# Where the operands of the products stand in SBUF: z's parts on even 64-byte lines, the key sums' parts on odd ones

## The chip, the cores and the metric

The kernel runs on one core of a Trainium2 chip. The metric is the device time of one execution in microseconds; the time before is the median of three runs. One further execution was profiled, and all rows come from that one.

## The reference

A graph layer, a linear-attention layer and a mixture of experts over 12500 nodes of 256 channels, in float32:

```python
xn = _layernorm(x)
x = x + gnn(xn, edges) + mix(xn)
x = x + ffn(_layernorm(x))
# gnn: xt = xn @ W; softmax over heads of gathered sums; weighted xt[col]
# mix: Q, K = elu(xn @ Wq) + 1, elu(xn @ Wk) + 1
#      KV = sum over nodes of K * v;  msg = (Q @ KV) / (Q . sum K) @ Wm, normalized
#      h = relu(concat(xn, msg) @ W1) @ W2;  mix = xn + layernorm(h)
# ffn: shared = relu(relu(y @ sW1 + b) @ sW2 + b) @ sW3 + b
#      4 experts of two hidden layers (eW1, eW2) and eW3, the best two weighted by a softmax
```

## The kernel before

**Tiling.** The 12500 nodes are cut into 25 groups (NG) of 512 nodes (GR), four row tiles of 128 each; the last group has two. Every large product is done in two-part float32r: a value is split into a high part (`..._hi`) and the rest (`..._lo`), and `split_mm` (L268 to L274) issues three matmuls for it, high x high (L272), high x low (L273), low x high (L274). The first argument of `pe.matmul` after the output is the operand that is loaded and held in the array (128 columns), the second the one that moves through it.

**Two kinds of product.** In one, a slice of the weights is held and 512 columns of nodes move: `hidden` (L541) and `w1_part` (L579). So run Wq and the first half of W1 on xT, the second half of W1 on mT (the message), sW1 and the four eW1 on z (the normalized middle result), sW2 on s1. In the other, 128 nodes are held and 256 columns move: W2 (`w2_pair`, L650) and eW3 (L745) with h held, sW3 (L740) with s2 held and out_bias (L739) with scaleT held, each against the weights, and `p2_m` (L569) with z held against g, the key sums folded with Wm. In profile rows the moving operand is named first: `psum<-z_hi,w_hi` has w_hi held and z_hi moving, `psum<-w_hi,h_hi` has h_hi held.

**Stages.** Phase 1 (L532) runs over the groups for the keys, the key sums and the gather table. Phase 2 (L680) is the second pass: one turn i works on three groups at a time, on the queries of group i (Wq, denominators, p2_m), the hidden layer of group i - 1 (W1, W2) and the experts of group i - 2. TensorE's order within a turn is written out by hand: transposes of row_n, W1's x half on the old xT buffer, outputs 2 and 3 (12 matmuls), Wq on the new one (12), W1's message half (12, then transposes of row_z, then 12), sW1, logits, denominators, sW1, eW1 (6 + 6 + 24 on z), W2 (48), sW2 (6), the second expert layer (8), the gates spread by gate_sel (2), p2_m (24), W1's x half for the next turn, outputs 0 and 1, on the new xT (12), the output stage (40). Every engine waits on semaphores; the other engines follow TensorE within the turn. There are two xT buffers, `xT_hi[0]`/`xT_lo[0]` (xT0) and `xT_hi[1]`/`xT_lo[1]` (xT1), used in turn; they are loaded by DMA from a table.

**Layout.** SBUF tiles are stacked one after another by `sb` (L70). It counts 64-byte lines per partition in `used[0]`; a tile with a `side` begins on a line whose number has that parity, if need be behind a filling line of 64 bytes:

```python
lines = -(-4 * math.prod(shape[1:]) // LINE)
if side is not None and used[0] % 2 != side:
    stack.enter_context(nc.sbuf_tensor(name + "_side", [P, LINE // 4], F32))
    used[0] += 1
made = stack.enter_context(nc.sbuf_tensor(name, shape, dt))
...
used[0] += lines
```

MOVING is 0 and HELD is 1. The weights w_hi and w_lo are on side 0, h, s2 and scaleT on side 1. z is on side 1 before, g on side 0; xT, s1, mT, gate_sel, den_sel and rdenT have no side of their own and stand where the tiles before them end. Starts in bytes per partition, added up from the tile sizes in the order of allocation:

| tile | before | within 256 | after | within 256 |
|---|---|---|---|---|
| w_hi / w_lo | 512 / 25088 | 0 | the same | 0 |
| gate_sel | 50688 | 0 | 50752 | 64 |
| second_w | 51968 | 0 | 52032 | 64 |
| g_hi / g_lo | 52992 / 55040 | 0 | 53056 / 55104 | 64 |
| xT_hi0 / xT_lo0 | 74880 / 78976 | 128 | 75008 / 79104 | 0 |
| xT_hi1 / xT_lo1 | 126976 / 131072 | 0 | 127104 / 131200 | 128 |
| row_n / row_z | 70784 / 88512 | 128 / 192 | 70848 / 88640 | 192 / 64 |
| e1 | 104896 | 192 | 105024 | 64 |
| s2_hi / s2_lo | 113088 / 178240 | 192 / 64 | 113216 / 178624 | 64 / 192 |
| den_sel / rdenT | 87488 / 115904 | 192 / 192 | 87616 / 116032 | 64 / 64 |
| h_hi / h_lo | 135232 / 143424 | 64 | 135360 / 143552 | 192 |
| z_hi / z_lo | 151616 / 155712 | 64 | 151808 / 155904 | 0 |
| s1_hi / s1_lo | 159808 / 163904 | 64 | 160000 / 164096 | 0 |
| scaleT | 168000 | 64 | 168256 | 64 |
| mT_hi / mT_lo | 170048 / 174144 | 64 | 170368 / 174464 | 128 |

Slices within a tile begin at multiples of 512 bytes, so each has its tile's place within 256.

Of the kernel before, what the change touches and what calls it, by code (L numbers as in the profile page):

```python
# [7 lines left out]
F32R = mybir.dt.float32r  # L8
# [6 lines left out]
C = 256  # L15
# [5 lines left out]
P = 128  # L21
R = 128
T = 4
GR = R * T
# [4 lines left out]
CK = C // P  # L29
BANK = 512  # L30
LINE, HALF_LINE = 64, 32
MOVING, HELD = 0, 1
XT_W = C + HEADS
XA_W = XT_W + HEADS
KX_W = C + 2
# [28 lines left out]
def gps_layer(nc, A):  # L64

    ctx = ExitStack()
    with ctx:
        used = [0]

        def sb(name, shape, dt=F32, stack=ctx, side=None):  # L70
# [6 lines that stand above are left out]
            if -(-4 * math.prod(shape[1:]) // HALF_LINE) % 2:  # L77
                stack.enter_context(nc.sbuf_tensor(name + "_fill", [P, HALF_LINE // 4], F32))
            used[0] += lines
            return made  # L80
# [46 lines left out]
        w_hi = sb("w_hi", [P, W_TOTAL], F32R, side=MOVING)  # L127
        w_lo = sb("w_lo", [P, W_TOTAL], F32R, side=MOVING)
        out_bias = sb("out_bias", [P, C], F32R, side=MOVING)
        gate_sel = sb("gate_sel", [P, 2, P], F32R)  # L130
        gate_w = sb("gate_w", [P, CK, QUAD])
        second_w = sb("second_w", [P, EXPERTS, HEAD_CH])
        g_hi = sb("g_hi", [P, CK, C], F32R, side=MOVING)
        g_lo = sb("g_lo", [P, CK, C], F32R, side=MOVING)
        g2_bc = sb("g2_bc", [R, C])
        b2_bc = sb("b2_bc", [R, C])
        h_bias = sb("h_bias", [P, 4])
# [29 lines left out]
        ctx0.close()  # L167
        used[0] = before_ctx0
        row_n = sb("row_n", [R, T, C])
        xT_hi0 = sb("xT_hi0", [P, CK, GR], F32R)  # L170
        xT_lo0 = sb("xT_lo0", [P, CK, GR], F32R)
        qf = sb("qf", [P, CK, GR])
        idx = [sb(f"idx{n}", [R, 2, T], I32) for n in range(2)]
        low_rows = sb("low_rows", [P, QUAD + 1])
        den_sel = sb("den_sel", [P, CK, P], F32R)

        ctx1, before_ctx1 = ExitStack(), used[0]
# [36 lines left out]
        s2_hi = sb("s2_hi", [P, GR], F32R, side=HELD)  # L215
        pad = sb("pad", [P, P])
        kden = sb("kden", [P, CK, QUAD])
        rdenT = sb("rdenT", [P, GR], F32R)
        rden_hi = sb("rden_hi", [P, R + 1], F32R)
        xg = [sb(f"xg{n}", [R, T, XT_W]) for n in range(2)]  # L220
        ag = [sb(f"ag{n}", [R, T, HEADS]) for n in range(2)]
        xT_hi = [xT_hi0, sb("xT_hi1", [P, CK, GR], F32R)]
        xT_lo = [xT_lo0, sb("xT_lo1", [P, CK, GR], F32R)]
        h_hi = sb("h_hi", [P, 4, GR], F32R, side=HELD)
        h_lo = sb("h_lo", [P, 4, GR], F32R, side=HELD)
        z_hi = sb("z_hi", [P, CK, GR], F32R, side=HELD)
        z_lo = sb("z_lo", [P, CK, GR], F32R, side=HELD)
        s1_hi = sb("s1_hi", [P, 2, GR], F32R)
        s1_lo = sb("s1_lo", [P, 2, GR], F32R)
        scaleT = sb("scaleT", [P, GR], F32R, side=HELD)  # L230
        mT_hi = sb("mT_hi", [P, CK, GR], F32R)
        mT_lo = sb("mT_lo", [P, CK, GR], F32R)
        s2_lo = sb("s2_lo", [P, GR], F32R, side=HELD)
        relu = [sb(f"relu{n}", [P, 2, GR]) for n in range(3)]
        gb_bc = sb("gb_bc", [R, EXPERTS])
# [1712 lines left out]
```

## Time and profile before

| what | value |
|---|---|
| median of 3 runs | 1325.66 us (1324.2 to 1329.84) |
| profiled execution | 1322.97 us, span 1321.1 us |
| TensorE (PE) busy | 1292.3 us, 98% |
| weight loads (PEld) busy | 1119.4 us |
| VectorE / ScalarE / GpSimd busy | 1105.4 / 733.8 / 770.7 us |
| matmuls | 8812 |
| one turn of phase 2 | 42.6 us, 22 turns |

Times are microseconds, means in a group nanoseconds. PE is the matmul engine, PEld its weight loads, which overlap with the matmuls. A matmul's duration includes its way through the array, so that consecutive ones overlap; the distance from one start to the next is the rate.

### The profile page before, as it was taken

How to read it: one execution, taken by the hardware profiler on the slowest of the kernel's cores; microseconds unless marked ns; L12 is line 12 of the kernel's file. 1: busy time of each engine (PE TensorE's matmuls, PEld its weight loads, DVE VectorE, ACT ScalarE, POOL GpSimd, SP SyncE). 2: the span in 40 equal slices, each digit the busy share in tenths (PEclk: the TensorE clock that was granted, in tenths of full speed). 3: DMA queues.
4: the chain of work that ended last, by engine and by line, in shares of the span. 5: the costliest groups of instructions: out<-in, count | busy, mean ns of one | idle time of the engine just before them, and what ended most of it. 6: DMA issues, size and time to landing. Idle time of an engine off the chain costs nothing.

```text
span 1321.1 us, 26301 instructions
## 1 busy us (share of the span) xinstructions
PE 1292.3 (98%) x8812; PEld 1119.4 (85%) x8812; DVE 1105.4 (84%) x2597; ACT 733.8 (56%) x1332; POOL 770.7 (58%) x815
## 2 busy tenths in 40 slices
PE   6999999899999999999999999999999999999998
PEld 5999999876888888888888888888888888888876
DVE  6988777978888888888888888888888888888875
ACT  4555555345645655455645655555645655555654
POOL 5777777745546654655556564655555654655531
PEclk9999999899999999999999999999999999999999
DMA  6787766523212221222111221222111221212000
GB/s 206 245 283 253 251 226 223 165 61 73 65 42 60 77 75 29 76 60 80 50 54 56 80 73 32 76 60 80 44 60 56 80 72 32 76 60 71 26 17 23
DMA packets 65459, 123.23 MB, mean 93 GB/s; under 512 B 31725, under 2 KB 36176, under 8 KB 65422
## 3 DMA queue, kind: packets, MB, share of 16 engines
q1 hardware_dynamic: 57422, 109.25, 25.6%
q0 software_dynamic: 8000, 13.53, 4.8%
q8 instruction: 19, 0.31, 0.1%
q14 instruction: 18, 0.15, 0.0%
HBM read 70.41 MB, written 52.32 MB: 93 GB/s over the span
## 4 chain that ended last, share of the span: by engine, by line
PE 88%; DVE 4%; issue 3%; POOL 2%; DVEq 1%; POOLq 1%; ACT 1%; ACTq 0%
PE psum L272 26%; PE psum L273 25%; PE psum L274 25%; PE psum L484 5%; PE psum L676 3%; PE psum L729 1%; PE psum L667 1%; PE psum L566 1%; PE psum L739 1%; PE psum L559 1%; POOL h_lo L1841 1%; POOL ag L1837 0%; POOLq L1775 0%; POOL xg L1835 0%; DVE kf L1249 0%
## 5 line engine op out<-in xcount | busy, mean ns | idle before, releaser
L1841 POOL TENSOR_TENSOR h_lo<-relu,h_hi 128x1024 fp32r<-128x1024 f32 (+1 forms) x50 | 119.8, 2397 | 142.1 <-ACT h_hi L998 142.0
L272 PE MATMUL psum<-w_hi,h_hi 128*128 128x256 f32 x588 | 164.4, 280 | 1.6 <-POOL h_lo L1841 1.5
L273 PE MATMUL psum<-w_lo,h_hi 128*128 128x256 f32 x588 | 163.8, 278 | 0.0
L274 PE MATMUL psum<-w_hi,h_lo 128*128 128x256 f32 x588 | 163.7, 278 | 0.0
L1841 POOL TENSOR_TENSOR s_lo<-relu,s_hi 128x512 fp32r<-128x512 f32 (+1 forms) x45 | 82.5, 1834 | 95.8 <-ACT s_hi L1099 94.3
L272 PE MATMUL psum<-z_hi,w_hi 128*128 128x512 f32 (+1 forms) x300 | 121.6, 405 | 2.0 <-DVE z_lo L1611 1.1
L1835 POOL DMA_INDIRECT xg<-table_xt,idx x100 | 99.5, 995 | 34.9 <-issue 31.9
L272 PE MATMUL psum<-xT_hi,w_hi 128*128 128x512 f32 (+1 forms) x300 | 119.4, 398 | 0.1
L997 ACT ACTIVATE relu<-psum,h_bias 128x512 f32<-128x512 f32 (+1 forms) x100 | 67.8, 678 | 88.5 <-PE psum L274 88.4
L273 PE MATMUL psum<-xT_lo,w_hi 128*128 128x512 f32 (+1 forms) x300 | 116.9, 390 | 0.0
L274 PE MATMUL psum<-xT_hi,w_lo 128*128 128x512 f32 (+1 forms) x300 | 116.7, 389 | 0.0
L273 PE MATMUL psum<-z_lo,w_hi 128*128 128x512 f32 (+1 forms) x300 | 116.6, 389 | 0.0
L274 PE MATMUL psum<-z_hi,w_lo 128*128 128x512 f32 (+1 forms) x300 | 116.2, 387 | 0.0
L272 PEld LDWEIGHTS psum<-w_hi,h_hi 128*128 128x128 f32 x588 | 110.4, 188 | 3.5 <-POOL h_lo L1841 1.9
L1837 POOL DMA_INDIRECT ag<-table_al,idx x100 | 95.2, 952 | 30.5 <-issue 30.5
L274 PEld LDWEIGHTS psum<-w_hi,h_lo 128*128 128x128 f32 x588 | 111.4, 190 | 0.0
L273 PEld LDWEIGHTS psum<-w_lo,h_hi 128*128 128x128 f32 x588 | 110.5, 188 | 1.0
L915 ACT ACTIVATE row_n<-psum,nm_m,rs_m 128x256 f32<-128x256 f32 x98 | 47.4, 564 | 111.4 <-POOL nm_m L1778 111.4
L1470 DVE SCALAR_TENSOR_TENSOR base<-xb,rn,b_bc 128x256 f32<-128x256 f32 x98 | 91.7, 975 | 0.2 <-issue 0.2
L1009 ACT ACTIVATE e<-psum,e_bias 128x512 f32<-128x512 f32 (+1 forms) x100 | 67.3, 676 | 37.2 <-PE psum L274 37.1
L272 PE MATMUL psum<-mT_hi,w_hi 128*128 128x512 f32 (+1 forms) x200 | 80.1, 401 | 0.9 <-DVE mT_lo L1619 0.9
L1811 POOL TENSOR_TENSOR k_lo<-kf,k_hi 128x1024 fp32r<-128x1024 f32 x25 | 63.0, 2521 | 30.3 <-DVE k_hi L1253 30.3
(274 smaller groups left out, 4298.1 us busy)
## 6 DMA issues: line engine op xcount, KB each, us to landing
xb<-in_x SPq DMA_DIRECT2D x47, 448.0 KB, 3.5
xT_hi_table<-x1T_hi SPq DMA_DIRECT2D x25, 512.0 KB, 2.8
xT_lo_table<-x1T_lo SPq DMA_DIRECT2D x25, 512.0 KB, 3.6
xT_hi<-xT_hi_table SPq DMA_DIRECT2D x25, 512.0 KB, 3.8
xT_lo<-xT_lo_table SPq DMA_DIRECT2D x25, 512.0 KB, 4.7
table_xt<-xts SPq DMA_DIRECT2D x24, 455.0 KB, 3.0
out<-xmid SPq DMA_DIRECT2D x24, 448.0 KB
xb<-in_x SPq DMA_DIRECT2D x47, 64.0 KB, 3.6
```

Source lines behind the costliest of these rows:

```text
L272: pe.matmul(out, wh, xh, start=first, stop=False)
L273: pe.matmul(out, wh, xl, start=False, stop=False)
L274: return pe.matmul(out, wl, xh, start=False, stop=last)
L484: last = pe.transpose(psum[:, b + c, j * R:(j + 1) * R], src[:, j, c * P:(c + 1) * P], ident[0:R, 0:R])
L915: act.activation(out[:, j, :], src(j), ACT.Identity, bias=nm[which][:, j:j + 1], scale=rs[which][:, j:j + 1]).then_inc(S[done], 1)
L997: act.activation(out[:, 0:t * R], colT(b, t=t), ACT.Relu, bias=bias)
L1009: act.activation(e1[:, e, 0:t * R], colT(bank, t=t), ACT.Relu, bias=e1_bias[:, e:e + 1]).then_inc(S["e1_relu"], 1)
L1470: last = stt(base[:, j, :], xb[par][:, j, :], rn2[par][:, 0, j:j + 1], b2_bc[:], ALU.mult, ALU.add)
L1811: ptt(k_lo[par][:], kf[par][:], k_hi[par][:], ALU.subtract).then_inc(S["k_split"], 1)
L1835: pool.indirect_dma_start(xg[par][:, j, :], None, table_xt.ap(), bass.IndirectOffsetOnAxis(idx[par][:, 1, j:j + 1], 0)).then_inc(S[f"gath{ ...
L1837: pool.indirect_dma_start(ag[par][:, j, :], None, table_al.ap(), bass.IndirectOffsetOnAxis(idx[par][:, 0, j:j + 1], 0)).then_inc(S[f"gath{ ...
L1841: ptt(out, src, hi, ALU.subtract).then_inc(S[done], 1)
```

## The change

It gives sides to tiles that had none and exchanges two. z_hi and z_lo go to side 0 and g_hi and g_lo to side 1; xT, s1 and mT are put on side 0, gate_sel, den_sel and rdenT on side 1. Filling lines come in or fall away, so that nearly all tiles behind gate_sel start 64 to 384 bytes later. No instruction is added, removed or reordered.

```diff
-MOVING, HELD = 0, 1
+MOVING, HELD, G_SIDE = 0, 1, 1
-        gate_sel = sb("gate_sel", [P, 2, P], F32R)
+        gate_sel = sb("gate_sel", [P, 2, P], F32R, side=HELD)
-        g_hi = sb("g_hi", [P, CK, C], F32R, side=MOVING)
-        g_lo = sb("g_lo", [P, CK, C], F32R, side=MOVING)
+        g_hi = sb("g_hi", [P, CK, C], F32R, side=G_SIDE)
+        g_lo = sb("g_lo", [P, CK, C], F32R, side=G_SIDE)
-        xT_hi0 = sb("xT_hi0", [P, CK, GR], F32R)
-        xT_lo0 = sb("xT_lo0", [P, CK, GR], F32R)
+        xT_hi0 = sb("xT_hi0", [P, CK, GR], F32R, side=MOVING)
+        xT_lo0 = sb("xT_lo0", [P, CK, GR], F32R, side=MOVING)
-        den_sel = sb("den_sel", [P, CK, P], F32R)
+        den_sel = sb("den_sel", [P, CK, P], F32R, side=HELD)
-        rdenT = sb("rdenT", [P, GR], F32R)
+        rdenT = sb("rdenT", [P, GR], F32R, side=HELD)
-        xT_hi = [xT_hi0, sb("xT_hi1", [P, CK, GR], F32R)]
-        xT_lo = [xT_lo0, sb("xT_lo1", [P, CK, GR], F32R)]
+        xT_hi = [xT_hi0, sb("xT_hi1", [P, CK, GR], F32R, side=MOVING)]
+        xT_lo = [xT_lo0, sb("xT_lo1", [P, CK, GR], F32R, side=MOVING)]
-        z_hi = sb("z_hi", [P, CK, GR], F32R, side=HELD)
-        z_lo = sb("z_lo", [P, CK, GR], F32R, side=HELD)
-        s1_hi = sb("s1_hi", [P, 2, GR], F32R)
-        s1_lo = sb("s1_lo", [P, 2, GR], F32R)
+        z_hi = sb("z_hi", [P, CK, GR], F32R, side=MOVING)
+        z_lo = sb("z_lo", [P, CK, GR], F32R, side=MOVING)
+        s1_hi = sb("s1_hi", [P, 2, GR], F32R, side=MOVING)
+        s1_lo = sb("s1_lo", [P, 2, GR], F32R, side=MOVING)
-        mT_hi = sb("mT_hi", [P, CK, GR], F32R)
-        mT_lo = sb("mT_lo", [P, CK, GR], F32R)
+        mT_hi = sb("mT_hi", [P, CK, GR], F32R, side=MOVING)
+        mT_lo = sb("mT_lo", [P, CK, GR], F32R, side=MOVING)
```

## Rows read from the trace of the kernel before

**Rows 1.** The page, sections 1 and 2: busy time; span in 40 slices.
```profile
...
PE 1292.3 (98%) x8812; PEld 1119.4 (85%) x8812; DVE 1105.4 (84%) x2597; ACT 733.8 (56%) x1332; POOL 770.7 (58%) x815
...
PEclk9999999899999999999999999999999999999999
...
```

**Rows 2.** Waits of PE: waiter, releaser, total us, times, longest.
```profile
...
PE psum L600 <- ACT xn L915: 9.2, 1, 9.2
PE psum L633 <- DVE kx L1359: 1.8, 1, 1.8
...
```

**Rows 3.** Window of one turn: length, PE, PEld, DVE, ACT, POOL busy.
```profile
...
682.30:724.90 42.60, 42.60 (x279) 35.85 (x277) 36.51 (x90) 24.09 (x43) 24.28 (x25) 1.00 0.22 62
...
```

**Rows 4.** Timeline of PE (start us, duration us): products on xT0.
```profile
...
683.36 0.39 PE L273 MATMUL psum<-xT_lo,w_hi 128*128 128x512 f32 x1
...
685.92 0.39 PE L272 MATMUL psum<-xT_hi,w_hi 128*128 128x512 f32 x1
...
```

**Rows 5.** The same: products on xT1, and the next group's first.
```profile
...
686.62 0.39 PE L272 MATMUL psum<-xT_hi,w_hi 128*128 128x512 f32 x1
...
688.43 0.39 PE L274 MATMUL psum<-xT_hi,w_lo 128*128 128x512 f32 x1
688.66 0.40 PE L272 MATMUL psum<-mT_hi,w_hi 128*128 128x512 f32 x1
...
```

**Rows 6.** The same: the first instruction behind the products on mT.
```profile
...
691.42 1.04 PE L484 MATMUL psum<-ident,row_z 128*128 128x128 f32 x8
...
```

**Rows 7.** The same: products on z, and the W2 stage behind.
```profile
...
700.75 0.39 PE L273 MATMUL psum<-z_lo,w_hi 128*128 128x512 f32 x1
...
701.91 0.39 PE L272 MATMUL psum<-z_hi,w_hi 128*128 128x512 f32 x1
...
704.66 0.28 PE L272 MATMUL psum<-w_hi,h_hi 128*128 128x256 f32 x1
...
710.32 0.27 PE L720 MATMUL psum<-ident,scale_rows 128*128 128x128 f32 x1
...
```

**Rows 8.** The same two turns on: W2's first start, next stage's first.
```profile
...
789.96 0.28 PE L272 MATMUL psum<-w_hi,h_hi 128*128 128x256 f32 x1
...
795.42 0.27 PE L720 MATMUL psum<-ident,scale_rows 128*128 128x128 f32 x1
...
```

**Rows 9.** Windows of 21 turns, instructions with h_hi only; columns as rows 3.
```profile
...
384.00:426.60 42.60, 8.57 (x49) 7.37 (x48) 1.26 (x2) 4.00 (x6) 4.81 (x2) 1.00 0.23 63
...
1193.20:1235.60 42.40, 8.39 (x49) 7.31 (x48) 1.26 (x2) 3.99 (x6) 4.80 (x2) 1.00 0.18 56
...
```

**Rows 10.** Groups of PE by shape: count, busy us, mean ns.
```profile
...
L272 PE MATMUL psum<-w_hi,h_hi 128*128 128x256 f32 x588 | 164.4, 280 | 1.6 <-POOL h_lo L1841 1.5
...
L272 PE MATMUL psum<-z_hi,w_hi 128*128 128x512 f32 x288 | 118.1, 410 | 1.7 <-DVE z_lo L1611 1.1 <-DVE z_lo L1507 0.6
...
L272 PE MATMUL psum<-w_hi,s_hi 128*128 128x256 f32 x98 | 27.2, 277 | 0.0
...
```

**Rows 11.** g_hi's products by tile, 21 turns: duration ns min/median/max.
```profile
...
L272 PE MATMUL psum<-g_hi,z_hi x168: 276/276/279, 373.9 to 1228.0; 128*128 128x256 f32 x168
...
```

**Rows 12.** Groups of PE by shape, as rows 10: the transposes.
```profile
...
L484 PE MATMUL psum<-ident,row_z 128*128 128x128 f32 x196 | 26.4, 274 | 1.6 <-ACT row_z L915 1.4
L484 PE MATMUL psum<-ident,row_n 128*128 128x128 f32 x196 | 26.2, 273 | 0.9 <-ACT row_n L915 0.9
...
```

**Rows 13.** Groups of DVE and POOL by shape: the low parts.
```profile
...
L1507 DVE TENSOR_TENSOR z_lo<-psum,z_hi 128x1024 fp32r<-128x1024 f32 x23 | 27.9, 1215 | 0.5 <-ACT z_hi L1033 0.5
...
L1811 POOL TENSOR_TENSOR k_lo<-kf,k_hi 128x1024 fp32r<-128x1024 f32 x25 | 63.0, 2521 | 30.3 <-DVE k_hi L1253 30.3
...
L1841 POOL TENSOR_TENSOR s_lo<-relu,s_hi 128x1024 fp32r<-128x1024 f32 x22 | 52.9, 2406 | 1.5
...
```

**Rows 14.** Durations by tile (ns min/median/max): xT0's, then xT1's stretch.
```profile
...
L273 PE MATMUL psum<-xT_lo,w_hi x3: 392/398/398, 684.1 to 685.5; 128*128 128x512 f32 x3
...
L274 PE MATMUL psum<-xT_hi,w_lo x3: 389/389/389, 687.1 to 688.4; 128*128 128x512 f32 x3
...
```

## The prediction

> **What bounds the kernel now.** The page comes first: TensorE (PE) is busy 98% of a span of 1321.1 us, at a granted clock of 9 tenths or more in every slice, the 2.4 GHz level [rows 1]. Then PE's own waits: after a start-up wait of 9.2 us the next is 1.8 us, and each occurs once or twice in the whole run [rows 2]. So the loop of the second phase, 22 turns of it, contains no wait of PE at all, and a turn shows it: 42.60 us, PE busy through all of it, VectorE 36.5, ScalarE 24.1, GpSimd 24.3 [rows 3]. A change in how fast PE starts its products therefore reaches the end one for one; VectorE has 6.1 us of slack in a turn, the others more.
>
> Durations can't be used for the sum, since products overlap: a 512-column one has 390 to 410 ns on the page but the next starts about 230 ns later. So I read start to start, over many products, from the timeline.
>
> **What the layout does now.** The sizes in the allocation give each tile's start. I write it within 256 bytes, weights against data; only differences matter. w_hi and w_lo stand at 0 and stay there. The two xT buffers differ: xT0 at 128 (start 74880), xT1 at 0 (126976). Both are "even", on the weights' side of 64 bytes. z, mT and s1 stand at 64, the other side. The same kind of product on each:
> - xT0 (distance 128): 683.36 to 685.92 is 11 starts, 2.56 us, 232.7 ns each [rows 4].
> - xT1 (distance 0): from 685.92 to 688.66 12 starts, 2.74 us, 228.3 with its first unsettled ones; settled, 686.62 to 688.43, 8 starts, 1.81 us, 226.3 [rows 4, 5].
> - mT (distance 64): 688.66 to 691.42 is 12 starts, 2.76 us, 230.0 [rows 5, 6].
> - z (distance 64): 700.75 to 704.66 is 17 starts, 3.91 us, 230.0; settled, 701.91 to 704.66, 229.2 [rows 7].
> Two buffers on the same side thus enclose the value of the other side: 228.3 and 232.7 around 230.0, or settled 226.3 and 232.7 around 229.2. Side alone is not what decides; the next bit up, 128 bytes, counts at least as much. This is the point on which I part from the change's own description.
>
> The 256-column products show a second thing, that one layout can run at two rates. W2's 48 products (h at 64 held, w at 0 moving, distance -64) take 5.66 us from 704.66 to 710.32, 117.9 ns each, in one turn [rows 7], and 5.46 us from 789.96 to 795.42, 113.8 each, two turns later [rows 8]; the durations are all 281 ns in the one and 276 in the middle of the other. That is most of the 0.1 to 0.2 us by which turns differ: weight loads with h_hi are busy for 7.36 or 7.37 us in 14 of the 21 turns from 341.5 us on and for 7.30 to 7.32 in 7, and these seven are the turns of 42.4 and 42.5 us, against 42.6 and 42.7 [rows 9]. I choose the reading that the end of the stage before decides, since nothing else differs between the turns.
>
> **The change, part by part.** Every tile after gate_sel moves, by 64 bytes at first and by 128 from xT_hi0 on, more behind z. By the allocation:
> - xT0 goes from distance 128 to 0 and xT1 from 0 to 128 (within 256). They exchange roles; each does 18 products in a mean turn. Cost 0.
> - z (36 products a turn) and s1 (6) go from 64 to 0: at xT1's 228.3 instead of 230.0 that is 42 x -1.7 = -71 ns a turn [rows 4, 5, 7].
> - mT (24 a turn) goes from 64 to 128: at xT0's 232.7, 24 x +2.7 = +65 ns a turn [rows 4, 5].
> - Together -6 ns a turn; 22 turns and the part turns at the ends, counted as 23, make -0.1 us. z's 288 products at L272, a third of its split ones, fit 12 a turn [rows 10].
> - z as the held operand of the key-sum product against g (24 of 256 columns) stays on opposite sides, as do h (72) and s2 against the weights; but all three turn the sign of the distance, -64 to +64 or back, within 256. No row shows a long run at +64. Nearest are s2_hi at +64 among -64s, mean 277 ns, against 276 for a settled g product and 280 for the mixed h ones [rows 10, 11]: at the fast rate. I take no change. Bounds: all W2 stages fast, 14 x 0.2 = -2.8 us; W2 always slow, 7 x 0.2 = +1.4 us, and with z/g and eW3 (48 a turn) slow too, 48 x 4.1 ns x 23 = +4.5 more, +5.9 in all [rows 7, 8].
> - gate_sel (2 products) goes onto scaleT's side and den_sel stays with rdenT: too few to count; at the 6.4 ns that separate xT0 and xT1 they are worth 0.3 us either way over the run [rows 4, 5]. The transposes hold row_n at 128 and row_z at 192 and take 273 and 274 ns: no sign of a preference [rows 12]. The 200 float32 products of second_w go from 192 to 0; at 6.4 ns each that is 1.3 us either way, and I take 0 [rows 4, 5].
> - The other engines read z, s1, mT, xb and row_n at new places. VectorE's z_lo has only z_hi in SBUF, 1215 ns; GpSimd's subtraction takes 2406 ns for s1_lo with both operands on one side and 2521 for k_lo with them on opposite ones [rows 13]. s1_lo becomes such an opposite pair: some 0.1 us more on an engine with 18 us of slack. If that cover were gone, it would cost 23 x 0.1 = 2.3 us. Nothing is added to any queue; no wait, transfer or instruction changes. Phase 1's matrices all shift by the same 128: 0.
>
> Sum: 0.0 to -0.1 us. The profiled execution took 1322.97 us, 1.9 beyond its span; the median of the runs is 1325.66, 2.7 above it, and I put the change on the median: 1325.5 us. Unknown costs alone reach from -2.8 - 1.5 (mT staying at 230: 24 x 2.7 ns x 23) = -4.3 to +5.9.
>
> One rule of the Trainium skill speaks against the change: TensorE: Matmul & The Clock Gate, "Step-by-step: what each phase is for", says TensorE reads SBUF through two independent ports, so that loading the next weights takes nothing from the running product. By that the layout is worth nothing and the time stays at the 1325.7 of before. Here the trace disagrees [rows 4, 5]: the same kind of product, weights at the same place within 256 bytes, two buffers, 6 ns apart.
>
> **Rivals.**
> - *The side is all that counts*, and a product with nothing unsettled before it keeps xT1's rate. For it: xT1, the fastest 512-column rate. Against: xT0 on the same side is the slowest. z, s1 and mT at 228.3: 66 x -1.7 x 23 = -2.6 us; with W2 always fast -5.4: 1320 to 1323.
> - *The 256-column products lock at the slow rate.* For: the slow rate holds in 14 of 21 turns [rows 9]. Against: g's products have a median of 276 ns, the fast kind's duration [rows 11]. +1.4 to +5.9: 1327 to 1331.5.
> - *Slower: collisions in 512-column products.* xT0's products last 392 and 398 ns, xT1's all 389 [rows 14]; if the mean start of 232.7 belongs to their mean of 395 and 226.3 to 389, the long ones stand near 236. It decides from 6.6 / 23 / 66 = +4.4 ns on each product. Against: chunks of weights 512 and 2048 bytes apart follow one another within each stage of [rows 4 to 7] with no mark in the starts.
> - *The layout acts on nothing measurable* (independent reads, the differences coming from phase alone): 1325.7. Against: the two xT stages stand back to back and differ by 4.4 ns a start even with the unsettled ones [rows 4, 5].
>
> **How the numbers follow.** A measurement of this kernel tells about 0.5%, 6.6 us, from no change. Forecast (1323 to 1327.5) 0.45, no effect 0.08, side alone 0.22, slow lock 0.15, collisions 0.07, something unseen that gains more 0.03. The range takes in forecast, side alone and the slow lock: 1320 to 1331.5. Faster by over 0.5% needs 6.6 us, more than the -5.4 of the best case: 0.04. Slower by over 0.5%: collisions and a corner of the lock, 0.09. Same: 0.87. The likeliest is 1325.5.
>
> **What would show it.** In the timeline after: z and s1 products settle at 226 to 227 ns start to start, mT at 232 to 233, the two xT buffers exchanged; turns still 42.4 to 42.7 us without PE waits. mT at 227 would prove the side rule; z above 229 would show that distance 256 is not distance 0; W2 at 114 in all turns or 118 in all would give the 256-column part. The forecast is wrong if a distance at which this kernel has no product now behaves unlike 0, 64 or 128.

## The result, and the profile after

The changed kernel takes 1335.92 us (median of 6 runs, 1333.74 to 1337.16). The kernel before, run beside it, takes 1327.41 over its six runs (1324.2 to 1329.84). The ratio is 1.0066, interval [1.0047, 1.0084]: slower by 8.5 us, where no change was forecast (1325.5, range 1320 to 1331.5). The profiled execution took 1337.16 us with a span of 1335.3, so 14.2 us more span than the one before.

The page after, busy time and granted clock (answers rows 1):

```profile
...
PE 1303.8 (98%) x8812; PEld 1130.2 (85%) x8812; DVE 1113.6 (83%) x2597; ACT 734.2 (55%) x1332; POOL 771.1 (58%) x815
...
PEclk9999999898999999999999999999999999999999
...
```

PE's waits after; waiter, releaser, total us, times, longest (answers rows 2):

```profile
...
PE psum L600 <- ACT xn L915: 9.1, 1, 9.1
PE psum L272 <- ACT e L1009: 3.0, 1, 3.0
PE psum L633 <- DVE kx L1359: 1.8, 1, 1.8
...
```

One wait is new, 3.0 us for ScalarE's `e`, once. PE is still busy 98%, with as many instructions. So most of the loss must lie in the starts. Windows of turn 11 after: the whole turn, then from the first start of W2, of the key sums and of the outputs (first product on out_bias) to the next stage's first start; columns as rows 3:

```profile
...
691.40:734.30 42.90, 42.90 (x277) 36.07 (x276) 36.63 (x89) 24.16 (x43) 24.14 (x25) 1.00 0.21 62
713.83:719.49 5.66, 5.66 (x50) 5.66 (x49) 4.37 (x20) 1.02 (x3) 4.60 (x5) 1.00 0.19 41
723.98:726.81 2.83, 2.83 (x26) 2.83 (x24) 1.96 (x4) 1.80 (x3) 2.01 (x4) 1.00 0.00 0
729.60:734.32 4.72, 4.72 (x41) 4.71 (x40) 4.38 (x13) 1.94 (x4) 1.24 (x2) 1.00 0.00 0
...
```

The same last two stages in turn 11 of the kernel before, which rows 7 don't show:

```profile
...
714.82:717.55 2.73, 2.73 (x25) 2.73 (x24) 1.96 (x4) 1.80 (x3) 1.91 (x4) 1.00 0.00 0
720.30:724.86 4.56, 4.56 (x41) 4.56 (x40) 4.30 (x13) 1.93 (x4) 1.24 (x2) 1.00 0.00 0
...
```

A turn has no wait in it, as before, and lasts 42.90 us where it lasted 42.60 [rows 3]. The key sums take 2.83 us for 24 starts where they took 2.73, the outputs 4.72 for 40 (the window begins 0.02 us apart) where they took 4.56. W2 takes 5.66, its slow value of [rows 7]; in none of the 21 full turns does it take the 5.46 of [rows 8]. The 512-column stages of that turn after, at the places of rows 4 to 7 (start us, duration us):

```profile
...
692.46 0.39 PE L273 MATMUL psum<-xT_lo,w_hi 128*128 128x512 f32 x1
...
694.99 0.40 PE L272 MATMUL psum<-xT_hi,w_hi 128*128 128x512 f32 x1
...
697.78 0.40 PE L272 MATMUL psum<-mT_hi,w_hi 128*128 128x512 f32 x1
...
700.59 0.38 PE L484 MATMUL psum<-ident,row_z 128*128 128x128 f32 x2
...
709.94 0.39 PE L273 MATMUL psum<-z_lo,w_hi 128*128 128x512 f32 x1
...
713.83 0.28 PE L272 MATMUL psum<-w_hi,h_hi 128*128 128x256 f32 x1
...
```

The old xT buffer, now xT0 at 0, takes 2.53 us for 11 starts, 230.0 ns each; the new one, xT1 at 128, 2.79 for 12, 232.5; mT 2.81 for 12, 234.2; z 3.89 for 17, 228.8. The groups by shape agree in direction, and would mislead alone, since products overlap (count, busy us, mean ns; answers rows 10; the last line answers rows 13):

```profile
...
L272 PE MATMUL psum<-w_hi,h_hi 128*128 128x256 f32 x588 | 165.8, 282 | 4.6 <-ACT e L1009 3.0 <-POOL h_lo L1841 1.5
...
L272 PE MATMUL psum<-g_hi,z_hi 128*128 128x256 f32 x196 | 54.9, 280 | 0.1
...
L272 PE MATMUL psum<-w_hi,s_hi 128*128 128x256 f32 x98 | 27.7, 283 | 0.0
...
L1841 POOL TENSOR_TENSOR s_lo<-relu,s_hi 128x1024 fp32r<-128x1024 f32 x22 | 52.9, 2406 | 1.8
...
```

Over the 21 full turns (turns 3 to 23), the mean turn goes from 42.577 to 42.935 us. Adding the trace's starts up by stage gives where the 0.358 us are, in ns a turn:

| stage | starts | before to after, ns a turn | forecast |
|---|---|---|---|
| xT, old, new, and behind the key sums | 35 | +23 | 0 |
| mT | 23 | +79 | +65 |
| z and s1, with what lies between | 42 | -45 | -71 |
| W2 (h held) | 48 | +66 | 0 |
| key sums (z held) | 24 | +91 | 0 |
| outputs (h, s2 held) | 40 | +155 | 0 |

These sum to 369; the rest of the turn gives back the difference. So 312 of these 369 ns are in the 256-column stages. The span's 14.2 us are 7.5 of these 21 turns, 6.1 of turn 2 alone, where the new wait is, and 0.6 elsewhere.

**Turn 2.** VectorE and GpSimd, kernel after (start us, duration us):

```profile
...
316.29 6.12 DVE L1516 TENSOR_TENSOR s_lo<-relu,s_hi 128x1024 fp32r<-128x1024 f32 x1 [0.52 <-ACT s_hi L998]
...
```

```profile
...
316.61 4.71 POOL L1841 TENSOR_TENSOR h_lo<-relu,h_hi 128x1024 fp32r<-128x1024 f32 x2
...
```

and the same two in the kernel before:

```profile
...
316.10 2.85 DVE L1516 TENSOR_TENSOR s_lo<-relu,s_hi 128x1024 fp32r<-128x1024 f32 x1 [0.52 <-ACT s_hi L998]
...
```

```profile
...
315.11 6.05 POOL L1841 TENSOR_TENSOR h_lo<-relu,h_hi 128x1024 fp32r<-128x1024 f32 x2
...
```

VectorE computes s1's low part from two operands in SBUF. The same subtraction took 1.22 us where GpSimd was not subtracting (in the run e8_seam, below). Here two subtractions of GpSimd run beside it, and it takes 2.85 us in one execution and 6.12 in the other. In the latter it starts 0.32 us before them and finishes only behind both: 0.32 + 4.71 + 1.22 = 6.25, near the 6.12. In the other GpSimd's two take 6.05 us instead of 4.71, so there VectorE's seems to have had its turn between them. The softmax behind it on VectorE is then late, ScalarE's `e` too, and PE stops for 3.0 us. After that stop the granted clock is lower; windows of the kernel after (granted clock is the column behind POOL):

```profile
...
325.00:330.00 5.00, 2.52 (x12) 2.52 (x13) 3.70 (x20) 1.02 (x3) 1.68 (x2) 0.66 0.14 29
330.00:335.00 5.00, 5.00 (x23) 4.47 (x22) 2.21 (x7) 1.72 (x6) 0.00 (x0) 0.65 0.01 3
...
```

The mean there is 0.66 and 0.65 of 2.4 GHz: most of the time at the 1.2 GHz level, 6.8 us of it without a break. Before, both windows read 1.00. The stop and half of those 6.8 us would be 3.0 + 3.4 = 6.4 us, an estimate against the 6.1 that turn 2 lost. The question that this leaves, and that the experiments answer, is whether the stall belongs to the change.

### The profile page after: what moved, and what is told of

Same layout as the page of the kernel before. It is cut to its first block, busy times and chain, and to the rows that moved or that the text cites. A ratio compares the mean times of both kernels' runs of the same rounds, so it can differ in the third digit from the quotient of the medians.

```text
span 1335.3 us, 26301 instructions
## 1 busy us (share of the span) xinstructions
PE 1303.8 (98%) x8812; PEld 1130.2 (85%) x8812; DVE 1113.6 (83%) x2597; ACT 734.2 (55%) x1332; POOL 771.1 (58%) x815
## 4 chain that ended last, share of the span: by engine, by line
PE 88%; DVE 4%; issue 3%; ACT 1%; POOL 1%; DVEq 1%; POOLq 1%; ACTq 0%
PE psum L272 25%; PE psum L274 25%; PE psum L273 25%; PE psum L484 5%; PE psum L676 3%; PE psum L729 1%; PE psum L667 1%; PE psum L566 1%; PE psum L739 1%; PE psum L559 1%; POOLq L1775 0%; DVE s_lo L1516 0%; POOL ag L1837 0%; POOL xg L1835 0%; DVE kf L1249 0%
```

## Experiments

The theory from the traces: the time from one product's start to the next depends on the place of both operands within 256 bytes, and for 256-column products also on what is ahead of them. The rivals: the side of 64 bytes is what counts; only the sign of the distance counts; the stall of turn 2 makes the difference. All kernels derive from the kernel before. In those with `PLACES`, `sb` puts a tile on the next 64-byte line whose number modulo 4 is the one named (0: the place of the weights, 1: 64 bytes on, 2: 128, 3: 192), and all operands of products that a diff does not name are where the kernel before has them, in e3 and e5 where the change puts them. Three chips were used: the first for e1 to e4 (the kernel before took 1326.82 us), a second for e5 to e8 (1342.92), a third for e9 to e12 (1342.82).

**e1_table.** Only products on copied data, 18 to a set, in the split pattern of the kernel; its output is not the reference's.

```python
for lead in ("float32", "products"):
    for cols in (512, 256):
        for distance in range(8):
            SETS.append((lead, cols, 0, distance))   # held at line 0, moving at line `distance`
for held, moving in ((1,0),(3,0),(3,2),(1,2),(0,3),(2,1),(2,3),(3,4)):
    SETS.append(("float32", 256, held, moving))
```

> A kernel of matmuls alone that computes nothing of the reference: 40 sets of 18 split products (float32r, 128 columns held), each set with its own place of the held and the moving operand in steps of 64 bytes, once behind four float32 products and once behind six 512-column ones; the output is a copy of x. Theory 'distance' (the rate hangs on moving minus held, within 256 bytes): 512 columns settle at 227 ns start to start at distance 0 and 256, 229 at 64 and 320, 233 at 128 and 384; 256 columns settle at 118 ns at +64 and 113 at -64 (192 and 448), whatever the absolute places, so that held 64 with moving 0 equals held 192 with moving 128. Rival 'which side is held' (256 columns are fast when the held operand is on an odd line): distances 64 and 192 run alike. Rival 'hand-over' (the stage before sets the rate): the sets behind float32 products and behind 512-column products differ, the distances don't.

Sets of 18 products of 512 columns behind float32 products, at distances 0 to 4 lines (start us, us of the set):

```profile
...
30.04 4.34 PE L53 MATMUL psum<-moving,held 128*128 128x512 f32 x18
...
35.03 4.38 PE L53 MATMUL psum<-moving,held 128*128 128x512 f32 x18
...
40.06 4.42 PE L53 MATMUL psum<-moving,held 128*128 128x512 f32 x18
...
45.12 4.45 PE L53 MATMUL psum<-moving,held 128*128 128x512 f32 x18
...
50.22 4.34 PE L53 MATMUL psum<-moving,held 128*128 128x512 f32 x18
...
```

The settled starts (the last nine of each set) are 226.7 ns at distance 0, 228.9 at 1, 232.1 at 2, 233.0 at 3, and 226.7 again at 4; 5 to 7 repeat 1 to 3. The period is 256 bytes. Behind other products they are within 1.2 ns of that. With 256 columns even distances give 118.8 to 120.2, odd ones either 117.8 or 113.3. Three odd pairs, (held, moving) = (3, 0), (3, 2) and (2, 3):

```profile
...
169.95 2.37 PE L53 MATMUL psum<-moving,held 128*128 128x256 f32 x18
...
172.96 2.29 PE L53 MATMUL psum<-moving,held 128*128 128x256 f32 x18
...
184.83 2.29 PE L53 MATMUL psum<-moving,held 128*128 128x256 f32 x18
...
```

The sets last 2.37, 2.29 and 2.29 us: 117.8, 113.3 and 113.3 settled. The pair at the place of h and w in the changed kernel, (3, 0), is slow here. Distances of +1 occur at both rates ((0, 1) slow, (2, 3) fast), and so do those of -1 ((1, 0) slow, (3, 2) fast); behind 512-column products, distance 5 gave 113.3 where 1 gave 117.8. So the place within 256 bytes is right for 512 columns; for 256 columns the distance and its sign decide nothing alone, beyond odd against even.

**e2_zg.** The exchange of z and g alone.

```diff
-    "g_hi": 0, "g_lo": 0, "z_hi": 1, "z_lo": 1,
+    "g_hi": 1, "g_lo": 1, "z_hi": 0, "z_lo": 0,
```

> The kernel before with z's and g's places alone exchanged (z at 0 and g at 64 within 256 bytes of the weights); h, s1, s2, mT, xT and all other matrices within 256 where they were. 'Distance': the key-sum stage goes from 114.0 to 117.8 ns a start (24 a turn, +92 ns), z's stages from 230.0 to about 229 (-40 ns), the output stage and mT stay at 114.1 and 230.0; a turn stays within 42.5 to 42.75 us. 'Hand-over': the output stage goes to 118 too and W2 is slow in all turns, a turn 42.8 us or more.

1326.04 us in one run, where the kernel before took 1320.18 to 1328.48 over 15: the time says nothing of an effect of 3 us, the trace does. Windows of turn 11: W2, key sums, outputs (columns as above):

```profile
...
705.69:711.35 5.66, 5.66 (x50) 5.65 (x49) 4.37 (x20) 1.02 (x3) 4.59 (x5) 1.00 0.22 51
715.85:718.67 2.82, 2.82 (x25) 2.82 (x24) 1.96 (x4) 1.80 (x3) 2.00 (x4) 1.00 0.00 0
721.42:725.99 4.57, 4.57 (x42) 4.57 (x41) 4.32 (x13) 1.93 (x4) 1.24 (x2) 1.00 0.00 0
...
```

W2 is slow in all 21 turns, not 14, and the key sums at 117.8 ns, 2.82 us. The outputs keep 4.57 here and take 18 ns more in the mean turn. Mean turn 42.711, +134 ns. So z at the weights' place locks W2 although h had not moved; for the key sums, whose own two operands are z and g, the stage ahead and the pair can't be told apart here. It gives somewhat over a third of the change's loss in a turn. Each of the two expectations got one half: W2 slow in all turns, but the outputs unharmed.

**e3_h.** The changed kernel's places with h and s2_lo back.

```diff
-    "h_hi": 3, "h_lo": 3, "s2_lo": 3,
+    "h_hi": 1, "h_lo": 1, "s2_lo": 1,
```

> The changed kernel with h and s2 alone moved, to 64 within 256 bytes, so that the weights stand at -64 from them as before. 'Distance': W2 falls from 117.8 to 113.8 ns a start (48 a turn) or at least to before's mixture, the output stage from 117.9 to about 114 (40 a turn), the key sums stay at 117.8; a turn falls from 42.93 to 42.58 us or to 42.65, the run by 6 to 8 us to 1328. 'Hand-over' and 'which side is held' (h is on an odd line in both): no change, 42.93 us a turn.

1332.7 us, 1.0053 [1.0031, 1.0075]. Turns of 42.832 us: W2 and key sums stay slow, the outputs run at 113.6 ns in 11 turns of 21 and at 117.8 in 10. Windows of the outputs in two turns that follow each other:

```profile
...
725.93:730.48 4.55, 4.55 (x41) 4.54 (x40) 4.29 (x13) 1.94 (x4) 1.24 (x2) 1.00 0.00 0
768.67:773.38 4.71, 4.71 (x41) 4.71 (x40) 4.41 (x13) 1.94 (x4) 1.24 (x2) 1.00 0.00 0
...
```

The shift of h and s2_lo, which comes only from the tiles ahead of them, thus makes the outputs slow in half of the turns; what is left of the change does so in the other half. 'Distance', which expected W2 to be fast again, fell.

**e4_all.** All 512-column operands at the fastest distance, what is held in 256-column products at an odd one.

```diff
+    "xT_hi0": 0, "xT_hi1": 0, "mT_hi": 0, "z_hi": 0, "s1_hi": 0,   # and their low parts
+    "g_hi": 3, "g_lo": 3, "s2_hi": 1, "gate_sel": 1,
```

> The layout that follows from the theory 'distance': xT, mT, z and s1 all at 0, h, s2 and scaleT at 64 and g at 192 within 256 bytes, weights at 0. 'Distance': all 512-column stages at 227 to 229 ns, all 256-column ones at 113.5 to 114; a turn of 42.25 us instead of 42.57, the run 7 us below the kernel before, ratio 0.995. 'Hand-over': a turn between 42.45 and 42.9 us as chance has it, ratio 1.000 to 1.006.

1330.8 us, 1.0032 [1.0018, 1.0046]: slower. The 512-column stages settle at 226.7 as the table has it, but W2, key sums and outputs all run at 117.8; a turn takes 42.705. This layout loses more in the 256-column stages than it gains in the others. Whether the 512-column places are to blame differs by stage: W2 is slow behind z at distance 0 in e2, e3 and here; the outputs stand behind xT at distance 0 in e6 and e11 too (below) and are fast there, with s2_hi at 192 instead of 64.

**e5_rest.** The changed kernel's places without the exchange of z and g.

```diff
-    "g_hi": 1, "g_lo": 1, "z_hi": 0, "z_lo": 0,
+    "g_hi": 0, "g_lo": 0, "z_hi": 1, "z_lo": 1,
```

> The changed kernel without its exchange of z and g: z at 64 and g at 0 within 256 bytes as before, all other tiles where the change puts them. If the cost of the change is the sum of its parts (the exchange alone gave +0.14 us a turn), this one has the rest: mT at 233 ns instead of 230 (+0.09 us), the output stage at 117.9 instead of 114.1 (+0.15 us), key sums back at 114.0; a turn of 42.80 us against 42.57 before and 42.93 after. If the slow output stage comes from what z and g hand on, the output stage is back at 114.1 and a turn has 42.65 us.

1345.22 us in one run; the kernel before on that chip 1342.92. Key sums fast in 20 of 21 turns, W2 and outputs slow in all: the outputs' loss does not come from z and g. The complement of e2.

**e6_512.** In the kernel before only xT0 and mT to the weights' place.

```diff
-    "xT_hi0": 2, "xT_lo0": 2, "mT_hi": 1, "mT_lo": 1,
+    "xT_hi0": 0, "xT_lo0": 0, "mT_hi": 0, "mT_lo": 0,
```

> The kernel before with xT0 and mT alone moved to distance 0 from the weights (xT0 from 128, mT from 64 within 256 bytes), all else of phase 2 where it was. By the table of e1_table 512-column products at distance 0 take 227 ns: xT0's 18 a turn gain 4.4 ns and mT's 24 gain 2.5, -0.14 us a turn and -3 us in the run (ratio 0.9977), if the 256-column stages keep their rates: output stage 114.1, key sums 114.0, W2 fast in a third of the turns. If a stage that has settled at distance 0 makes the 256-column stage behind it slow, the output stage, which stands behind xT's products, goes to 117.8 in all turns: +0.15 us a turn and no gain.

1341.87 us, 0.9989 [0.9978, 0.9999]. Wq 226.7, mT 227.5, and W2 is now fast in all 21 turns, which was not expected. The outputs, now behind xT at distance 0 in every turn, stay fast in all 21: the other case of the expectation did not come about. But the run gained less than that is worth, since PE waits in every turn of it:

```profile
...
PE psum L762 <- ACT relu L1129: 11.8, 21, 0.6
...
```

This wait for ScalarE's relu is not in [rows 2]. Against e8_seam's turn on the same chip W2 takes 122 ns less and the products on xT and mT 138 less, but the second expert layer, where the wait is, 148 more. The wait comes from a late signal. The transpose of the gates (L720 in these line numbers) and the copy of its result by ScalarE, in e8_seam on the same chip:

```profile
...
764.23 0.27 PE L720 MATMUL psum<-ident,scale_rows 128*128 128x128 f32 x1
...
```

```profile
...
765.58 0.27 ACT L1003 ACTIVATE scaleT<-psum 32x128 fp32r<-32x128 f32 x1 [3.51 <-PE psum L720]
```

and ScalarE in the kernel before, whose transpose started at 752.94:

```profile
...
753.25 0.27 ACT L1003 ACTIVATE scaleT<-psum 32x128 fp32r<-32x128 f32 x1 [2.48 <-PE psum L720]
```

The copy starts 1.35 us behind the transpose's start against 0.31 (0.31 in all turns 3 to 23 of the five profiles of the first chip, before, after and e2 to e4; 1.23 to 1.58 in these turns of all seven full kernels on the other two). VectorE, waiting for the product behind the transpose, idles 1.23 us there against 0.39. In e8_seam the lag is 1.28 to 1.37 us where W2 was slow and 1.46 to 1.56 where it was fast: as if the copy waited for a fixed point in the turn, so that what W2 gains up to there is hidden. What holds the two engines isn't known; it was not tried apart. The wait is in all seven traces of these two chips. Of the kernel before itself none was kept there; e8_seam is the nearest to it. Six of the seven (not e12) have one more wait ahead of the loop, 4.0 to 5.1 us near 270 us, for VectorE's z_lo, where the kernel before has none over 1.1.

**e7_handover.** Products alone, again, the output not the reference's. For each of the eight odd pairs of e1's question: 18 products of 256 columns directly behind a row of 512-column products, at distance 0, 1 or 2, in rows of 18, 19 or 20.

```python
for distance, count in ((0, 18), (1, 18), (1, 19), (1, 20), (2, 18)):
    for held, moving in ((1,0),(3,0),(1,2),(3,2),(0,1),(2,1),(0,3),(2,3)):
        SETS.append(("wide", distance, count, ((18, held, moving),)))
```

> Matmuls alone, nothing of the reference computed, the output a copy of x: 18 products of 256 columns with held and moving operand in all eight pairs of opposite 64-byte lines within 256, behind (a) 18 products of 512 columns at distance 0, (b) 18, 19 and 20 at distance 64, (c) 18 at distance 128, (d) two at the gates' places; then the output stage's own order of places behind (a) and (c). 'Hand-over': a pair is not fast or slow by itself, but settles at 113.3 or 117.8 ns by what stands before it; behind (b) about one of three lengths is fast for a given pair, behind (a) W2's pairs (held 64 or 192, moving 0) are slow. 'Distance with sign': +64 and -64 differ in all surroundings.

Windows from a set's first start to the next product: pair (1, 0) behind distance 0, the same pair behind distance 1, pair (3, 0) behind distance 1:

```profile
...
33.45:35.57 2.12, 2.12 (x20) 2.12 (x18) 0.00 (x0) 0.00 (x0) 1.00 0.00 0
83.26:85.33 2.07, 2.07 (x20) 2.07 (x19) 0.00 (x0) 0.00 (x0) 1.00 0.03 8
89.44:91.57 2.13, 2.13 (x20) 2.12 (x19) 0.00 (x0) 0.00 (x0) 1.00 0.00 0
...
```

| ahead | pairs of 8 settling at 113.3 ns |
|---|---|
| 18 at distance 0 | 0 |
| 18, 19, 20 at distance 1 | 3, 1, 1 |
| 18 at distance 2 | 2 |
| two at the gates' places, before and after | 4, 3 |

One more product ahead, nothing else different, turns pair (2, 3) from 113.3 to 117.8. Behind distance 0 no pair is fast. For W2 that is e2 and e4 without the kernel around them. A rate, once settled, held to the end of its set. Of eight longer sets, cut into parts of a few products, six switched between held lines: they went over to 113.3 on the way and stayed; the two that kept one pair stayed at 117.8.

The pair matters beside what is ahead, more than was expected ("about one of three lengths is fast for a given pair"). Counted by pair over the seven surroundings:

| pair (held, moving) | in the kernel | fast of 7 |
|---|---|---|
| (1, 0) | W2 and key sums before | 5 |
| (3, 0) | W2 after | 0 |
| (0, 1) | key sums after | 0 |
| (2, 1), (3, 2), (0, 3), (2, 3), (1, 2) | - | 4, 3, 1, 1, 0 |

So the change took both stages from the pair that is most often fast to pairs that were never fast here. The six switching sets show that (3, 0) can run at 113.3 once the rate is there.

**e8_seam.** The kernel before, with the subtraction that runs beside GpSimd's moved behind the first half of the softmax chain in turn 2.

```diff
-                    dve.wait_ge(S["s1_relu"], 2 * (i - 1))
-                    tt(s1_lo[:], relu[2][:], s1_hi[:], ALU.subtract).then_inc(S["s1_lo"], 1)
...
                     soft_chain_in(i, par, a, c)
+                    if second:
+                        dve.wait_ge(S["s1_relu"], 2 * (i - 1))
+                        tt(s1_lo[:], relu[2][:], s1_hi[:], ALU.subtract).then_inc(S["s1_lo"], 1)
```

> The kernel before with one step of one turn moved: in turn 2 VectorE makes s1_lo (both operands in SBUF) after the softmax's first part instead of before the denominators. In the changed kernel's profile that step takes 6.12 us beside GpSimd's subtractions instead of 2.85, PE then waits 3.0 us in turn 2 and runs 6.8 us at half clock. If most runs of the kernel before have this stall too, the median falls by about 3 us or more (1323.5) and every run has a clock of 0.997 or more. If the stall belongs to the changed layout alone, no change: 1326.8.

1339.62 us, 0.9971 [0.9961, 0.9981]: 3.3 us. The moved subtraction, by tile (duration ns min/median/max):

```profile
...
L1521 DVE TENSOR_TENSOR s_lo<-relu,s_hi x1: 1217/1217/1217, 327.1 to 327.1; 128x1024 fp32r<-128x1024 f32 x1
...
```

It takes 1217 ns, and no stop of PE there is longer than 0.94 us. The size is the expected one. The clock is not: 0.995 to 0.997 in these runs, where 0.997 or more was expected of every one. The 3.3 us say that the kernel before loses to the stall as well on this chip; no trace of it was kept there. The nearest is e6_512, on the same chip and without this edit, where the subtraction takes 3.83 us and PE then stands for 2.8 us:

```profile
...
L1549 DVE TENSOR_TENSOR s_lo<-relu,s_hi x1: 3828/3828/3828, 325.3 to 325.3; 128x1024 fp32r<-128x1024 f32 x1
...
```

The kernel before's own profile, on the first chip, shows 2.85 us and no stop of PE.

**e9_after and e10_after_seam.** The changed kernel again, and with the edit of e8_seam.

> The changed kernel once more, beside the next run and on its chip. Theory one (the loss is the loop's: 256-column products at 117.8 ns instead of 113.3 in the second-layer, key-sum and output stages, and the early stall in turn 2 is a matter of luck that both kernels share): 1.005 to 1.007 of the kernel before. Theory two (turn 2's stall, 6.1 us in the profiled run, belongs to the change and makes most of the difference of the medians): the next run, which takes the stall's cause away in both, shows a far smaller distance than this one.

> The changed kernel with the subtraction of s1's low part in turn 2 moved behind the softmax chain's first half, as e8_seam did with the kernel before (it measured 0.9971 of it). Theory one: the stall was shared, so this is 0.997 of the changed kernel, 1.003 to 1.004 of the kernel before, and turns 3 to 23 are what they were (42.9 us each, second-layer and key-sum products at 117.8 ns). Theory two: it comes to within 0.001 of e8_seam's ratio, 0.996 to 0.998 of the kernel before.

1347.66 us, 1.0036 [1.0022, 1.005], and 1344.42, 1.0007 [0.9998, 1.0016]. Both are below theory one's ranges, 1.005 to 1.007 and 1.003 to 1.004. What decides between the theories is what the edit does in each kernel: it gives 3.2 us here and gave 3.3 in the kernel before, and e10 against e8, each by the ratio to the kernel before on its own chip, differ by 0.0036, as e9 from the kernel before. On these two chips the stall is shared, theory one. That the distance is 0.0036 and not 0.0066 is for the most part the late signal: PE waits for it in each turn of e9, e10 and e8, less where its own stages are slower,

```profile
...
PE psum L729 <- ACT relu L1096: 6.2, 21, 0.3
...
```

0.30 us a turn in e9 against 0.41 in e8_seam. Of the +358 ns of a turn on the first chip +228 are left (43.256 against e8_seam's 43.028): W2 brings 76, the key sums 70, the outputs 156, and the stage with the wait gives back 115. The key sums are fast in 3 of the 21 turns of e9 and in 8 of e10's, against none on the first chip.

On the first chip the edit was not tried. There the subtraction takes 6.1 us in all three profiles with xT and mT moved (after, e3, e4) and 2.8 in the two without (before, e2), so its length may hang on the layout. But there too the loop's 7.5 us leave at most 1.0 of the 8.5 between the medians.

**e11_512_seam.** The edits of e6 and e8 together.

> The two edits that measured faster, together, in the kernel before: node and message operands of the 512-column products at the weights' place within 256 bytes (e6_512, whose 256-column stages ran at 113.5 to 114 ns but whose PE then waited about 0.5 us more behind the second layer, since the signal after the transpose of the gates came 1.0 to 1.2 us late on that chip), and the moved subtraction (e8_seam). If the late signal is that chip's and not the layout's: on a chip without it a turn of 42.29 us against 42.56, 1316 to 1320 us where the kernel before takes 1327 (0.993 to 0.996); on one with it 0.996 of the kernel before. If the two stages lock at 117.8 here, about 0.998.

1336.65 us, 0.9952 [0.9938, 0.9965]: 6.2 us faster than the kernel before. Windows of its turn 11, W2, key sums, outputs:

```profile
...
713.26:718.72 5.46, 5.46 (x49) 5.45 (x48) 4.17 (x19) 1.02 (x3) 4.40 (x5) 1.00 0.18 39
723.80:726.53 2.73, 2.73 (x25) 2.73 (x24) 1.98 (x8) 1.98 (x5) 1.81 (x4) 1.00 0.00 0
729.28:733.85 4.57, 4.57 (x42) 4.57 (x41) 4.31 (x11) 1.93 (x4) 1.31 (x3) 1.00 0.00 0
...
```

All three are at the fast rate, W2 and outputs in 21 turns of 21, key sums in 19. Mean turn 42.881, with 0.53 us of the wait for the late signal in it. It was not run on a chip without that.

**e12_shift.** In the kernel before only W2's and the output stage's operands h and s2 where the change pushed them.

```diff
-    "h_hi": 1, "h_lo": 1, "s2_hi": 3, "s2_lo": 1,
+    "h_hi": 3, "h_lo": 3, "s2_hi": 1, "s2_lo": 3,
```

> The kernel before with one part of the change alone: the second layer's operands where the added fills pushed them (h and the low part of s2 at 192 of 256 bytes, the high part of s2 at 64); z, g, the node, message and first-layer operands stay. Theory one (what locks a 256-column stage is the rest of its operands modulo 256 bytes together with the phase of the stage ahead of it): the second layer at 117.8 ns in every turn and the outputs at 117.9, as in e5_rest which had these and the others without z and g; key sums stay at 113.5 to 114; a turn 42.56 + 0.04 + 0.15 = 42.75 us, 1.003 of the kernel before. Rival (the odd distance's sign is of no importance and only z at the weights' own place locks them): all three stages stay as in the kernel before and so does the time.

1344.98 us, 1.0017 [1.0008, 1.0027]. Windows of its turn 11, W2, key sums, outputs:

```profile
...
714.46:720.11 5.65, 5.65 (x49) 5.64 (x48) 4.36 (x20) 1.02 (x3) 4.59 (x5) 1.00 0.20 42
724.99:727.71 2.72, 2.72 (x26) 2.72 (x24) 1.96 (x8) 1.97 (x5) 1.81 (x4) 1.00 0.00 0
730.45:735.17 4.72, 4.72 (x41) 4.71 (x40) 4.46 (x13) 1.94 (x4) 1.32 (x3) 1.00 0.00 0
...
```

W2 5.65 us in every turn, outputs 4.72, key sums 2.72 in this turn and fast in 16 of 21: theory one, though the turn grew by 0.138 us and not 0.19, since the wait hides W2's part.

**The hand-over in the kernel.** The starts in the trace show what goes with W2's rate. The interval from the last product on z to W2's first, against the rate of the 47 starts behind it, in turns 3 to 23:

| kernel | h at | interval 225 to 229 ns | interval 235 or 236 ns |
|---|---|---|---|
| before | 64 | 14 turns, all slow | 7 turns, all fast |
| e8_seam | 64 | 13, all slow | 8, all fast |
| after, e9_after, e10_after_seam | 192 | 63, all slow | none |
| e2_zg, e3_h, e4_all | 64 | 63, all slow | none |
| e6_512, e11_512_seam | 64 | none | 42, all fast |

At z's distance of 64 the starts repeat a cycle of three, near 226, 229 and 232 ns, and where in the cycle the stage ends varies from turn to turn; at distance 0 they repeat 226, 227, 227 and the end is always the same. With h at 192 (e5_rest, e12_shift) the intervals are 230 to 238 and W2 is slow in all 42 turns: the pair counts beside the phase. What the engine does in those ten nanoseconds no view shows.

The interval is no rule for other stages. Before the outputs, from the last product on xT to the first on out_bias, with h, s2_hi and s2_lo at the places named:

| kernel | h, s2_hi, s2_lo at | interval 225 to 227 ns | interval 229 to 232 ns |
|---|---|---|---|
| before, e6, e8, e11 | 64, 192, 64 | 84 turns, all fast | none |
| e2_zg | 64, 192, 64 | 11, all fast | 10, all fast |
| e3_h | 64, 64, 64 | 10, all slow | 11, all fast |
| e4_all | 64, 64, 64 | 21, all slow | none |
| after, e9, e10 | 192, 64, 192 | 36, all slow | 27, all slow |
| e5_rest, e12_shift | 192, 64, 192 | 42, all slow | none |

With s2_hi at 192 and h at 64 the outputs are fast behind any end that occurred, xT at distance 0 or 128; with s2_hi at 64 the end decides; with h at 192 they are slow behind all. e3 and e4 differ from the kernel before in other places too, so that it is s2_hi and not one of these was not tried alone.

## Why the prediction was wrong

- **What bounds the kernel: right.** No wait of PE in turns 3 to 23, and a turn's starts reach the end one for one, on the first chip. On the two others a wait once a turn hides part.
- **xT0 and xT1 exchange roles, cost 0: right in kind.** As the new buffer their starts went from 227.9 and 232.7 to 228.3 and 232.6. The stages around brought +23 ns a turn, 0.5 us.
- **z and s1, -71 ns: -45.** z settles at 226.7 as forecast (e1: 226.7 against 228.9). But the stage is cut by other products, and the first ten or so starts behind each cut run at about 231. The step read a settled value into unsettled starts.
- **mT, +65 ns: +79.** 233.5 a start, part of it unsettled; the forecast had 232.7.
- **256-column products, "I take no change": the step that failed.** It measured +312 ns a turn, some 6.9 us over 22 turns. The reason given was the "nearest row", s2_hi at +64 with 277 ns. But that row's products stand between h's in the output stage, which was fast as a whole in all 21 turns; it could say nothing of a stage whose operands all stand at +64. For W2 the prediction had named a right cause of its two rates, "the end of the stage before decides", and moved z, that stage, without asking what end it would now have: at distance 0 W2 was slow in every full turn (e2, e3, e4). And the turned sign, put at nothing, is enough without it: h and s2 moved alone make W2 and the outputs slow in all turns (e12), and in e7 the new pairs of W2 and of the key sums were slow in seven surroundings of seven, where the old one was fast in five.
- **The bound was too near as well.** 48 products for key sums and outputs left out sW3's and out_bias's; there are 64 starts. At the measured 3.8 to 3.9 ns each that is 5.4 us instead of 4.5.
- **The rival "lock at the slow rate", 1327 to 1331.5, is what happened.** Its upper end of +5.9 measured 6.9; with mT's +1.7, xT's +0.5 and z's -1.0 that is 8.1 us for 22 turns, and the medians are 8.5 apart. The rest of the miss of 10.4 us: the 1325.66 that it was added to was the median of three runs, and six give 1327.41, 1.75 more. The rival's full price on top of that, 1333.3, would still have been below the 1335.92.
- **s1_lo on GpSimd, 0.1 us more for operands on opposite sides: nothing.** Its mean is 2406 ns before and after, so opposite sides alone do not make k_lo's 2521 [rows 13].
- **The stall of turn 2 was not foreseen, and the ratio doesn't come from it.** It makes 6 of the 14 us between the two profiled executions, 3.2 to 3.3 us of each kernel's median on the other two chips, and nothing of the ratio there (e8, e10); on the first chip at most 1.0 us is left for it.
- **Rivals that fell.** The side alone: distance 2 lines is 5.4 ns slower than 0 (e1). Collisions at 236 ns: the slowest settled start is 233.7 (e1). No effect at all: the Trainium skill, TensorE: Matmul & The Clock Gate, "Step-by-step: what each phase is for", has loads and moving reads on independent ports. Here the same product starts every 226.7 to 233.7 ns by place alone (e1), so the measurement decides against taking the places for worth nothing.

For the stall, the Trainium skill, SBUF — State Buffer, "SBUF: two separate sides", says that a VectorE operation with two inputs in SBUF and a GpSimd one that reads SBUF take a shared port pair in turns, each for a whole instruction. This case agrees that one waits for the other: 6.12 us holds GpSimd's 4.71 and 1.2 of its own, and away from them it takes 1217 ns. How the turns are given out it leaves open: VectorE's record starts 0.32 us ahead of both subtractions and ends behind both.

## What to carry to other kernels

Where TensorE has no waits, read starts, not durations, and compare layouts with the phase in mind: a stage can run at one of two rates for all of its products, and the places of its own operands and the end of the stage ahead pick it together. A layout that is best for one kind of product can leave the next kind at its slow rate (z at distance 0 and W2: e2, e4), and another nearly as good can leave it fast (e11), so measure all stages of a turn, and treat fills ahead of a tile as a change to every tile behind it. Before putting a difference between two profiled executions down to the change, look whether one stretch makes it alone; here the largest piece in one place was a stall that the kernel before has too.

## Of the hardware, not expected

- Starts of 512-column products by the operands' distance: 226.7, 228.9, 232.1 and 233.0 ns at 0, 64, 128 and 192 bytes, then again from 256 (e1).
- 256-column products on odd distances have two stable rates, 113.3 and 117.8 ns; on even ones 118.8 to 120.2. Once fast they stayed fast, also where pairs were switched (e7). Of the eight pairs (1, 0) was fast in five surroundings of seven, three others in none (e7).
- Two of the three chips took 16 us longer for the same kernel. The loop there has a release of ScalarE and VectorE about 1.0 us later in each of turns 3 to 23 (0.8 us for VectorE). It costs PE 0.3 to 0.6 us a turn, 6.0 to 11.8 in the run, and six of seven traces have a wait of 4.0 to 5.1 us ahead of the loop besides; the cause of both stays open.
